# A recurrence of 64 chunks: TensorE's loop closes behind the attention matmuls, the last gradient operations work in two halves, transposes write in place

## What is computed

```
def step(carry, inp):
    W1c, b1c = carry
    xq, xk, xv, et = inp
    Z1 = xk @ W1c + b1c
    grad = _ln_l2_bwd(Z1, xv - xk, g, bb)
    Attn1 = jnp.tril(xq @ xk.swapaxes(-1, -2))
    b1_bar = b1c - jnp.tril(et) @ grad
    Z1_bar = xq @ W1c - et * Attn1 @ grad + b1_bar
    last_eta = et[..., -1, :, None]
    W1n = W1c - (last_eta * xk).swapaxes(-1, -2) @ grad
    b1n = b1c - (last_eta * grad).sum(-2, keepdims=True)
    return ((W1n, b1n), xq + _ln(Z1_bar, g, bb, EPS_IN))
```

## Time and profile before

| what | us |
| --- | --- |
| median of three runs (580.4, 584.08, 591.69) | 584.08 |
| the profiled execution's own time | 581.06 |
| its span | 579.2 |
| busy in it: PE 483.9, DVE 432.1, ACT 346.2, POOL 327.8 | |

### The profile page before, as it was taken

The page is one execution under the profiler, slowest core; times in us unless marked ns, Lnnn a source line. Parts: engine busy times, 40 slices in busy tenths (PEclk is TensorE's granted clock), DMA queues, the critical chain, the costliest instruction groups (busy, mean ns, idle before and its releaser), DMA issues.

```text
span 579.2 us, 30352 instructions
## 1 busy us (share of the span) xinstructions
PE 483.9 (84%) x12556; PEld 313.8 (54%) x12556; DVE 432.1 (75%) x1526; ACT 346.2 (60%) x1166; POOL 327.8 (57%) x590
## 2 busy tenths in 40 slices
PE   0699889898558789888888888888887699998996
PEld 0344334443346577777777676666675244456563
DVE  4757788888746789888888888888885667676652
ACT  2344334322246788888888889988885487553321
POOL 1276888787734466666666655565763667330112
PEclk9999989899858999999999999999997899998998
DMA  8310111111101011111111000011010500000123
GB/s 338 123 24 14 37 37 36 38 36 36 39 9 32 22 37 28 33 32 33 33 28 37 1 1 1 19 36 37 19 37 4 171 1 2 1 2 1 74 75 145
DMA packets 15136, 24.74 MB, mean 43 GB/s; under 512 B 4228, under 2 KB 4968, under 8 KB 15080
## 3 DMA queue, kind: packets, MB, share of 16 engines
q1 hardware_dynamic: 15080, 24.10, 13.8%
HBM read 11.50 MB, written 4.19 MB: 27 GB/s over the span
## 4 chain that ended last, share of the span: by engine, by line
PE 25%; DVE 24%; ACT 12%; issue 8%; POOL 2%; POOLq 0%; ACTq 0%
PE PS L1167 6%; PE PS L924 4%; PE PS L1255 3%; PE PS L906 3%; ACT work L1556 3%; PE PS L361 2%; DVE work L1341 2%; DVE work L1336 2%; DVE work L1322 2%; DVE work L1300 2%; DVE work L1319 2%; DVE PS L1338 2%; DVE PS L1323 2%; DVE PS L1302 2%; DVE PS L1325 2%
## 5 line engine op out<-in xcount | busy, mean ns | idle before, releaser
L1167 PE MATMUL PS<-work 32*32 32x32 f32 x4064 | 59.6, 194 | 37.9 <-DVE work L1341 21.0
L1167 PEld LDWEIGHTS PS<-work 32*32 32x32 f32 x4064 | 53.8, 108 | 43.4 <-issue 43.1
L1411 POOL TENSOR_TENSOR work<-work,mask 128x256 f32<-128x256 f32 x64 | 46.8, 731 | 35.7 <-ACT work L1531 35.7
L512 PE MATMUL PS<-X,work 128*128 128x512 f32 x128 | 63.2, 641 | 0.3 <-ACT X L435 0.3
L1423 POOL TENSOR_TENSOR work<-work,lrh 128x4 f32<-128x4 f32 x64 | 12.9, 201 | 75.6 <-DVE work L1314 70.1
L1300 DVE TENSOR_REDUCE work<-work 128x4 f32<-128x128 f32 x64 | 18.3, 286 | 49.2 <-ACT work L1556 49.2
L663 POOL TENSOR_TENSOR work<-work 128x512 f32<-128x512 f32 x32 | 43.8, 1370 | 7.1 <-DVE work L582 7.1
L1152 PEld LDWEIGHTS PS<-work 64*32 64x32 f32 x2048 | 32.9, 110 | 24.9 <-issue 23.6
L1152 PE MATMUL PS<-work 64*32 64x64 f32 x2048 | 43.6, 225 | 2.9 <-issue 2.0
L1194 PE MATMUL PS<-cst 128*128 128x256 f32 x126 | 45.1, 440 | 0.0
L1179 PE MATMUL PS<-work 32*64 32x32 f32 x2016 | 43.0, 222 | 2.2 <-issue 2.2
(11 more groups left out here) (162 smaller groups left out, 1344.5 us busy)
## 6 DMA issues: line engine op xcount, KB each, us to landing
X<-in_x SPq DMA_DIRECT2D x4, 1024.0 KB, 8.2
TK<-KP SPq DMA_DIRECT2D x64, 64.0 KB, 1.9
X<-QP SPq DMA_DIRECT2D x64, 64.0 KB, 2.0
TK<-in_x SPq DMA_DIRECT2D x16, 256.0 KB, 3.0
out<-TK SPq DMA_DIRECT2D x16, 256.0 KB, 2.4
work<-in_rope SPq DMA_DIRECT2D x2, 512.0 KB, 9.1
cst<-in_consts SPq DMA_DIRECT2D x1, 289.0 KB, 5.0
work<-in_wk SPq DMA_DIRECT2D x1, 256.0 KB, 11.2
```

The costliest lines, as they stand in the source:

```text
L512: mm = nc.tensor.matmul(PS[:, 2 + m, :], lhs(j), xt(i, j), start=(j == 0), stop=(j == J - 1))
L1167: mm = nc.tensor.matmul(PS[HD * a:HD * a + HD, bank, b * width:b * width + HD], AM[p][HD * a:HD * a + HD, b, part, :, :].rearrange("p e t ...
L1411: nc.gpsimd.tensor_tensor(AM[p].rearrange("p b s e t -> p (b s) e t"), S1[p].unsqueeze(2).broadcast_to([P, 2 * B, E, CS]), mask2.rearrange ...
```

## The change

On TensorE the body is cut into `front` (corrections, update, attention, filler) and `back` (next base, base queries). Chunk 0 has a back only; the fronts of chunks 1 and 2 and the back of chunk 1 are written out ahead of the loop, the loop runs back and front four times a turn, and the last front in the loop has no filler. The corrections wait for two semaphores in turn: `gla` for batches 0 and 1, `gl` for batches 2 and 3. On DVE, WX and GL are each made in two halves of the batches. The transpose writes TT itself, ZT and ACT's copies are gone, and so are the waits on them.

```
-                def body(c, p):
+                def front(p, before, done, now, fill):
                     o = 1 - p
-                    done, now, nxt = value(pe, c), value(pe, c + 1), value(pe, c + 2)
-                    before = value(pe, c - 1) if past(c, 2) else None
-                    if past(c, 1):
-                        pe.wait_ge(q["init"], 1)
-                        pe.wait_ge(q["gl"], done)
-                        pe.wait_ge(q["am"], done)
-                        pe.wait_ge(q["s1"], now)
-                        grads(ZW, ZB[p], o, 1).then_inc(q["corr"], 1)
...
+                    pe.wait_ge(q["gla"], done)
+                    pe.wait_ge(q["am"], done)
+                    pe.wait_ge(q["s1"], now)
+                    grads(ZW, ZB[p], o, 1, range(0, B // 2))
+                    pe.wait_ge(q["init"], 1)
+                    pe.wait_ge(q["gl"], done)
+                    grads(ZW, ZB[p], o, 1, range(B // 2, B)).then_inc(q["corr"], 1)
...
+                    update(o)
+                    grads(HD, QB[o], o, 0, range(B)).then_inc(q["attn"], 1)
+                    if fill:
+                        if before is not None:
                             pe.wait_ge(q["zq"], before)
                         filler(p)
-                    else:
-                        base(0, 0, 1, 1)
+                def back(c, p, before, now, nxt):
                     if not is_last(c):
-                        base(c + 1, o, nxt, now)
+                        base(c + 1, 1 - p, nxt, now)
...
-                run_chunks(pe, body)
+                base(0, 0, 1, 1)
+                back(0, 0, None, 1, 2)
+                front(1, None, 1, 2, True)
+                back(1, 1, None, 2, 3)
+                front(0, 1, 2, 3, True)
+                with nc.Fori(0, NC // 4 - 1, engines=(mybir.EngineType.PE,), hint_back_edge=True) as four:
+                    for k in range(4):
+                        c, p = four * 4 + (2 + k), k % 2
+                        before, done, now, nxt = (value(pe, c + n) for n in (-1, 0, 1, 2))
+                        back(c, p, before, now, nxt)
+                        front(1 - p, done, now, nxt, k < 3)
+                back(NC - 2, 0, NC - 3, NC - 1, NC)
+                front(1, NC - 2, NC - 1, NC, True)
+                back(NC - 1, 1, NC - 2, NC, None)
...
-                    nc.vector.transpose(ZT.rearrange("p b d -> p (b d)"), ZN.rearrange("p b d -> p (b d)")
-                                        ).then_inc(q["zt"], 1)
+                    nc.vector.transpose(
+                        TT.rearrange("p e (b n) -> p b e n", b=B)[:, :, :, c * CS:(c + 1) * CS],
+                        ZN.rearrange("p b (e t) -> p b e t", e=E)).then_inc(q["ot"], 1)
...
-                    nc.vector.tensor_tensor(WX, ZC, bc(cc1), ALU.mult).then_inc(q["w"], 1)
-                    dve.wait_ge(q["w"], c + 1)
+                    halves = slice(0, B // 2), slice(B // 2, B)
+                    for h in halves:
+                        nc.vector.tensor_tensor(WX[:, h, :], ZC[:, h, :], bc(cc1[:, h]), ALU.mult).then_inc(q["w"], 1)
                     dve.wait_ge(q["yc"], c + 1)
-                    nc.vector.tensor_tensor(GL[p], WX, YC, ALU.add).then_inc(q["gl"], 1)
+                    for k, h in enumerate(halves):
+                        dve.wait_ge(q["w"], 2 * c + 1 + k)
+                        nc.vector.tensor_tensor(GL[p][:, h, :], WX[:, h, :], YC[:, h, :], ALU.add
+                                                ).then_inc(q["gl" if k else "gla"], 1)
...
-                        pool.wait_ge(q["zt"], c + 0)
+                        pool.wait_ge(q["ot"], c + 0)
...
-                def out_store(c):
-                    act.wait_ge(q["zt"], c + 1)
-                    nc.scalar.activation(
-                        TT.rearrange("p e (b n) -> p e b n", b=B)[:, :, :, ds(c * CS, CS)],
-                        ZT.rearrange("p b (e t) -> p e b t", e=E), ACT.Copy).then_inc(q["ot"], 1)
...
```

More of the change, by code:

```diff
@@ L760, in build @@
         ZQ = [carve(B, HD) for _ in range(3)]
-        SQQ, ZN, ZT = (carve(B, HD) for _ in range(3))
+        SQQ, ZN = (carve(B, HD) for _ in range(2))
         ss, sz, ssq, sd1 = (carve(B) for _ in range(4))
@@ L1098, in build @@
             names = ("init my cy updw wcopy bcopy kt2 qt2 qr kr khx base qbase corr s1 am p sq ss sz zc v sd r ts y yp m u u2 "
-                     "yl c w yc gl upd attn zq sqq ssq sdq rq zn zt ot").split()
+                     "yl c w yc gla gl upd attn zq sqq ssq sdq rq zn ot").split()
             q = {n: sem(f"scan_{n}") for n in names}
@@ L1112, in past @@
                 return c >= n if isinstance(c, int) else n <= 2
[L1114 to L1122, removed]
             GAIN_AT, PRE_AT = NC // 2 + 8, NC - 8
@@ L1161, in base, with grads @@
                         ).then_inc(q["base"], 1)
-                def grads(width, bank, p, part):
-                    for b in range(B):
+                def grads(width, bank, p, part, batches):
+                    for b in batches:
                         for a in range(4):
@@ L1195, in filler @@
                                      skip_group_check=True)
-                def body(c, p):
+                def front(p, before, done, now, fill):
                     o = 1 - p
-                    done, now, nxt = value(pe, c), value(pe, c + 1), value(pe, c + 2)
-                    before = value(pe, c - 1) if past(c, 2) else None
-                    if past(c, 1):
-                        pe.wait_ge(q["init"], 1)
-                        pe.wait_ge(q["gl"], done)
-                        pe.wait_ge(q["am"], done)
-                        pe.wait_ge(q["s1"], now)
-                        grads(ZW, ZB[p], o, 1).then_inc(q["corr"], 1)
[L1208 to L1213, removed]
+                    pe.wait_ge(q["init"], 1)
[3 more added lines that the diff above has]
+                    grads(ZW, ZB[p], o, 1, range(0, B // 2))
+                    pe.wait_ge(q["init"], 1)
+                    pe.wait_ge(q["gl"], done)
+                    grads(ZW, ZB[p], o, 1, range(B // 2, B)).then_inc(q["corr"], 1)
+                    pe.wait_ge(q["init"], 1)
+                    pe.wait_ge(q["khx"], done)
+                    pe.wait_ge(q["bcopy"], done)
+                    update(o)
+                    grads(HD, QB[o], o, 0, range(B)).then_inc(q["attn"], 1)
+                    if fill:
+                        if before is not None:
                             pe.wait_ge(q["zq"], before)
                         filler(p)
-                    else:
-                        base(0, 0, 1, 1)
+                def back(c, p, before, now, nxt):
                     if not is_last(c):
-                        base(c + 1, o, nxt, now)
+                        base(c + 1, 1 - p, nxt, now)
                     else:
@@ L1224, in body @@
                     pe.wait_ge(q["wcopy"], now)
-                    if past(c, 2):
+                    if before is not None:
                         pe.wait_ge(q["zq"], before)
@@ L1233, in body @@
                                     QT2[p][r:r + 64, k * B + b, :, :].rearrange("p e t -> p (e t)"),
-                                    R[o][r:r + 64, k, b, 0:HD], start=(b == 0), stop=False,
+                                    R[1 - p][r:r + 64, k, b, 0:HD], start=(b == 0), stop=False,
                                     skip_group_check=True)
                     mm.then_inc(q["qbase"], 1)
-                run_chunks(pe, body)
+                base(0, 0, 1, 1)
[12 more added lines that the diff above has]
+                back(NC - 1, 1, NC - 2, NC, None)
                 pe.wait_ge(q["gl"], NC)
                 pe.wait_ge(q["am"], NC)
-                grads(HD, QB[1], 1, 0).then_inc(q["attn"], 1)
+                grads(HD, QB[1], 1, 0, range(B)).then_inc(q["attn"], 1)
                 def project(i, first):
@@ L1354, in _ @@
                 out_var(NC - 2)
-                dve.wait_ge(q["ot"], NC - 4)
                 out_turn(NC - 4)
@@ L1361, in _ @@
                 out_r(NC - 1)
-                dve.wait_ge(q["ot"], NC - 3)
                 out_turn(NC - 3)
@@ L1365, in _ @@
                 dve_scale(dve, 0)
-                dve.wait_ge(q["ot"], NC - 2)
                 out_turn(NC - 2)
-                dve.wait_ge(q["ot"], NC - 1)
                 out_turn(NC - 1)
@@ L1556, in body @@
                     nc.scalar.activation(SQ, zb, ACT.Square).then_inc(q["sq"], 1)
-                    if past(c, 5):
-                        out_store(c - 5)
                     if past(c, 2):
@@ L1615, in _ @@
                 out_square(NC - 2, 0)
-                out_store(NC - 5)
                 out_sd(NC - 2, 0)
-                out_store(NC - 4)
                 out_square(NC - 1, 1)
@@ L1622, in _ @@
                 out_sd(NC - 1, 1)
-                out_store(NC - 3)
                 act_square(act, 1, False)
                 act_affine(act, 0)
-                out_store(NC - 2)
```

(1 more changed line is left out.)

## The result

| | before | changed |
| --- | --- | --- |
| median, 20 executions each | 583.53 us | 594.16 us |
| ratio, 95% interval | 1 | 1.0141, 1.0108 to 1.0173 |
| span of the profile | 579.2 us | 600.9 us, in a second one 591.6 us |

The changed kernel's executions spread from 585.62 to 602.75 us. The first profile is the longest execution, so a second one, of 593.41 us, stands beside it.

The account below looks back on a forecast made before the run. Bound taken: DVE's chain plus one hop over PE and ACT. Halves 4.2, turn 4.4, chunk 58 0.7, loop's end 1.9, start 0 sum to 11.2 us: span 579.2 to 568.0, time 570.0 us, range 564 to 579.

Parts of the forecast that it names:

- The clock: At the loop's turn, PE without a filler falls to 1.2 GHz, 14 times 1.83 us: 595 us; rival, chance 0.04.
- the signs that would prove the forecast wrong: Plain chunks at 4.07 us or more, or a clock under 1.00 or code transfers between 212 and 345 us.
- The halves: WX and GL split on DVE: corrections 0.11 us earlier in each of 38 plain chunks, 4.2 us gained.
- plain chunk: One of 38 recurrence chunks bound by DVE's chain plus a PE and ACT hop: 4.06 to 4.07 us, forecast about 3.96.
- chunk with a gain: Chunks 41 to 48, with an extra ACT operation: they wait for S1, stay at 4.585 us and gain nothing.
- The turn: TensorE's loop turn moves behind attention, without filler: ten chunks of 4.47 to 4.54 us become 4.06, 4.4 us gained.
- S1 binds there: In chunks with a turn S1, not GL, releases the corrections, 4.06 us after the last ones; halves add nothing.
- The loop's end: Stop behind TensorE's loop comes earlier in the chunk; 5.3 less 2.4 less 1.0 gives 1.9 us gained, bounds 0 and 3.2.
- the count of 75 instructions: With code blocks of 256, about 75 instructions are left after the loop, nearly all of the next base.
- no transfer within the loop: TensorE's loop: code transfers from 212 to 345 us would disprove the forecast; fetch rival, 614 us, chance 0.03.
- no gain from the transposes: Transposes write runs of 16 directly and 64 ACT copies go; ACT waits for DVE's sum anyway: 0 us.
- a chunk 58 with 0.6 us less: Chunk 58's corrections wait for the loop's turn; without it they load at 420.07 instead of 420.73: 0.7 us gained.

Follow-up runs that it names:

- filler at the turn: The changed kernel with the filler put back at the loop's turn, so all four fronts have one: 582.23 us, ratio 0.996 to the kernel before.
- whole: The changed kernel with WX, GL and the corrections whole again, still without a filler at the turn: 591.17 us, ratio 1.0155 to the kernel before.

## Why the prediction was wrong

It gave 570.0 us, 564 to 579, and faster; the time is 594.16 and slower.

- **The clock, a rival with a chance of 0.04, is what happened.** Its mechanism and place were right, and a clock under 1.00 between 212 and 345 us was among the signs that would prove the forecast wrong. The step that failed is the sentence against it, that the gap at the turn is as long as before and the clock stayed at 1.00 then. It looked at the length of one standstill. The old loop with one filler less has that same gap of 0.84 us and falls; the filler of 16 columns leaves everything but the work, and falls. The filler's own cost was counted (0.67 us saved at the turn) and its use was not. That the rival's 595 us comes so near to 594.16 is luck: it is 14 falls of 1.83 us less gains of 11.2, and three to six falls came, of 2.3 to 4.7 us in the second profile, while most of the gains did not. Without the falls the kernel takes 582.23 us (0.996), which is still above the range: the other terms were too large as well.
- **The halves: 0.11 us a plain chunk were worked out, 0.02 came.** The durations held: 225 ns for a 128x64 WX against the 0.23 interpolated, starts 0.14 apart. Two waits had been charged at nothing. GL waits for two semaphores and starts 0.33 us behind WX, not 0.28, so that the corrections' loads start at 0.63, not 0.58 (0.69 before); with one wait less on DVE they start at 0.55, as the experiment shows. And the loads now take 0.42 us instead of 0.37, which eats most of what was left. They do not wait for the second GL half there. In a chunk with a gain (filler at the turn) both halves of GL end at 375.76, and the loads, 0.53 us later, are as slow:

```profile
375.40 0.36 DVE L1351 TENSOR_TENSOR work<-PS,work 128x64 f32<-128x64 f32 x2
...
376.29 0.41 PEld L1157 LDWEIGHTS PS<-work 32*32 32x32 f32 x32 [0.62 <-issue]
```

  So TensorE's second wait itself is the likely cause; no run removes it alone, and it is not shown. It also costs 0.045 in each chunk with a gain, where nothing had been charged. With the DVE wait gone the period is 3.97, close to the 3.96 forecast.
- **The turn: 0.85 us were carried over to the new place, 0.94 to 1.02 came**, so 4.17 us (whole) and 4.22 to 4.30 (halves) instead of 4.06. Why the standstill is longer there stays open. The ten turns before took 45.04; at 4.17 the saving is 3.3, at 4.26 2.4, not 4.4. That S1 binds there, as foreseen, is shown by PE's corrections being released by it:

```profile
329.90 0.51 PE L1157 MATMUL PS<-work 32*32 32x32 f32 x32 [0.16 <-ACT work L1538]
```

- **The loop's end: the place was right, the price of what follows was not.** The stop came behind the base's last load, as the count of 75 instructions said (second profile, base's bias, then the queries; answers to the earlier trace rows):

```profile
449.67 0.30 PEld L1148 LDWEIGHTS PS<-work,cst 128*128 128x128 f32 x2
452.92 0.55 PEld L1223 LDWEIGHTS PS<-work 64*32 64x32 f32 x32 [2.95 <-issue]
```

  Chunks 62 and 63 take 11.08 us instead of 13.48. But the slow clock that used to fall on chunks 62 and 63 now reaches into the work behind the recurrence. The first ten microseconds behind the last chunk's start, before and in the second profile (columns as above; the clock is 1.00 and 0.63):

```profile
447.27:457.27 10.00, 6.67 (x146) 3.56 (x138) 6.31 (x27) 5.19 (x19) 6.61 (x10) 1.00 0.52 168
```
```profile
454.56:464.56 10.00, 7.47 (x134) 4.27 (x130) 5.86 (x28) 3.54 (x13) 4.72 (x8) 0.63 0.63 218
```

  That work takes 137.0 us instead of 131.9: 5.1, where 1.0 was charged. In this pair the 1.9 us forecast as a gain are a loss of 2.7. Over all kept profiles, chunks 62 and 63 and what follows take 145.4 to 147.0 us in the four with the old loop and 146.0 to 148.1 in the eight with the new one, so the gain did not come, and the size of the loss is not sure. The second block's mean, which answers to the earlier trace rows, shows the wait in the first profile, released by DVE, not by POOL, and at a low clock:

```profile
474.06 3.11 PE L361 MATMUL PS<-TK,cst 128*128 128x512 f32 x4 [2.21 <-DVE TK L368]
```

- **Right:** no transfer within the loop on the queue that carried TensorE's code in the first pass (q8; from 212 to 345 us only q14 carries code, as before), no gain from the transposes, chunks with a gain bound by ACT, and a chunk 58 with 0.6 us less (5.11 against 5.70).

## What to carry to other kernels

A matmul that computes nothing is not free time to be taken away: here the clock fell when it went. That a gap of the same length did no harm in the kernel before was no proof, since that gap had the filler near it. A filler in front of the branch cost almost nothing here, and behind it some 0.4 us a turn (4.21 against 4.59). When an operation is split to let a consumer start early, count the waits on both engines: here 0.06 us on DVE and, as it seems, 0.05 on TensorE ate most of a gain of 0.11, and joining two semaphores on DVE gave most of it back.

## What the runs showed of the hardware

- The clock's falls are not regular: of the 13 turns with the same instructions among chunks 10 to 61, three fall in the second profile, and six falls stand in the first, mostly at other turns. A single profile of such a kernel says little about its time (585.62 to 602.75).
- One 128 x 256 f32 matmul a turn (0.70 us on PE) divides the kernels into two groups. With it in every chunk, the mean clock of an execution is 0.938 to 0.962 (42 executions of five experiments); without it, or with 16 columns, it is 0.889 to 0.939 (46 executions of the changed kernel and three experiments).
- At the turn of TensorE's loop the weight loads stand still for 0.84 to 1.02 us, though no code moves on q8 there. The register moves for the waits lie in the same time; the branch's own share is not known.
- A wait on DVE for a semaphore that is long reached, put between two dependent operations, cost 0.06 us.
